# A selective-scan kernel: pair sums one step later, and loop rounds of four chunks in place of two

## What is computed

```python
def step(hst, inputs):
    ut, dt, bt, ct = inputs
    dA = jnp.exp(dt[..., None] * A)
    hst = hst * dA + (dt * ut)[..., None] * bt[:, :, None, :]
    y = jnp.einsum('bkdn,bkn->bkd', hst, ct)
    return (hst, y)
```

## Time and profile before

| | us |
|---|---|
| median of 3 runs | 35231.98 |
| their range | 35160.76 to 35288.79 |
| the profiled execution | 35258.12 |
| span of its trace | 35256.3 |
| the four scans in it, together | 21998 |

### The profile page before, as it was taken

One profiled execution on the slowest core, in us unless ns is written; L12 is line 12 of the kernel. 1 busy time (PEld: TensorE's weight loads), 2 busy tenths in 40 slices (PEclk: granted clock), 3 DMA queues, 4 the chain that ended last, 5 costly groups with the idle time before them and its releaser, 6 DMA issues. The chain is left out here.

```text
span 35256.3 us, 353348 instructions
## 1 busy us (share of the span) xinstructions
PE 26406.9 (75%) x100774; PEld 8372.0 (24%) x100774; DVE 24871.2 (71%) x15541; ACT 15127.5 (43%) x20404; POOL 21995.5 (62%) x9902
## 2 busy tenths in 40 slices
PE   7857888885547788888876668888873758888884
PEld 3422222221223322222223222222211322222221
DVE  1237999997322289999981269999983139999995
ACT  1044555553233345555511345555541245555551
POOL 0016999996000089999930149999980029999991
PEclk8857888887667778888867668888876768888887
DMA  1022122213212222221243221222124232122214
GB/s 67 10 116 77 40 48 47 48 42 102 80 67 96 97 52 48 48 47 40 47 151 122 105 87 43 44 47 45 42 61 159 94 110 44 43 47 48 47 42 147
DMA packets 928980, 2422.06 MB, mean 69 GB/s; under 512 B 113744, under 2 KB 331668, under 8 KB 919504
## 3 DMA queue, kind: packets, MB, share of 16 engines
q1 hardware_dynamic: 927000, 2398.76, 24.4%
HBM read 1375.34 MB, written 1023.05 MB: 68 GB/s over the span
## 5 line engine op out<-in xcount | busy, mean ns | idle before, releaser
L1086 POOL TENSOR_TENSOR scan_hc<-scan_bc,scan_h 128x1024 f32<-128x1024 f32 x6912 | 16089.6, 2352 | 716.1 <-DVE scan_h L1248 712.5
L1248 DVE TENSOR_TENSOR_SCAN scan_h<-scan_da,scan_state,scan_dbu 128x1024 f32<-128x1024 f32 x6912 | 15983.3, 2335 | 246.4 <-ACT scan_da L1138 237.8
L1169 PE MATMUL scan_da<-scan_dd,scan_ssel 32*128 32x512 f32 x27648 | 9456.1, 776 | 2807.7 <-DVE scan_h L1248 2610.9
L1138 ACT ACTIVATE scan_da<-scan_da,scan_a_cur 128x1024 f32<-128x1024 f32 x6912 | 7517.9, 1088 | 8291.5 <-PE scan_da L1169 8286.9
L1169 PE MATMUL scan_p_du<-scan_dd,scan_ssel 32*128 32x512 f32 x27648 | 9670.6, 781 | 657.9 <-DMA scan_bc<-bc_d 197.7
L1235 DVE TENSOR_TENSOR scan_dbu<-scan_p_du,scan_bc 128x1024 f32<-128x1024 f32 x4608 | 5553.9, 1205 | 1008.8 <-PE scan_p_du L1169 986.4
L1072 POOL TENSOR_TENSOR scan_dbu<-scan_bc,scan_dus 128x1024 f32<-128x1024 f32 x2304 | 5420.9, 2353 | 154.5 <-ACT scan_dus L1112 148.4
L1169 PEld LDWEIGHTS scan_da<-scan_dd,scan_ssel 32*128 32x128 f32 x27648 | 2562.4, 224 | 10345.9 <-DVE scan_h L1248 8310.3
L1186 PE MATMUL scan_p_y<-scan_hc,scan_rsel 128*32 128x512 f32 x27648 | 4930.3, 795 | 6.7 <-POOL scan_hc L1086 6.7
L1169 PEld LDWEIGHTS scan_p_du<-scan_dd,scan_ssel 32*128 32x128 f32 x27648 | 2491.8, 219 | 3817.4 <-DVE scan_dbu L1235 2937.0
L856 PE MATMUL prep_p_dt<-prep_dtv,prep_wdt 12*128 12x384 f32 x2304 | 1449.3, 789 | 1930.7 <-DVE prep_delta L914 1730.8
(11 more groups left out here) (202 smaller groups left out, 13865.8 us busy)
## 6 DMA issues: line engine op xcount, KB each, us to landing
scan_bc<-bc_d SPq DMA_DIRECT2D x576, 512.0 KB, 12.3
du_d<-prep_du SPq DMA_DIRECT2D x384, 576.0 KB, 2.8
delta_d<-prep_delta SPq DMA_DIRECT2D x384, 576.0 KB, 3.7
scan_dd<-delta_d SPq DMA_DIRECT2D x1152, 192.0 KB, 4.8
scan_dd<-du_d SPq DMA_DIRECT2D x1152, 192.0 KB, 6.6
y_d<-scan_y SPq DMA_DIRECT2D x576, 384.0 KB, 5.1
merge_y<-y_d SPq DMA_DIRECT2D x384, 576.0 KB, 3.8
xs_d<-proj_xs_o SPq DMA_DIRECT2D x96, 588.0 KB, 3.4
```

The source lines that it names most:

```text
L1086: nc.gpsimd.tensor_tensor(hc[:, u % HC_SLOTS, :], c, h[:, u % H_SLOTS, :], ALU.mult).then_inc(hc_ready, 1)
L1138: nc.scalar.activation(da[u % DELTA_BANKS][:], da[u % DELTA_BANKS][:], ACT.Exp, scale=a_cur[:, u // UNITS, u % UNITS:u % UNITS + 1]).then_ ...
L1169: return nc.tensor.matmul(dst[:, half * H:(half + 1) * H], ssel[rows, i, :], dd[rows, s, m, j, :], start=True, stop=True)
L1248: nc.vector.tensor_tensor_scan(h[:, v % H_SLOTS, :], da[v % DELTA_BANKS][:], dbu[:, v % DBU_SLOTS, :], state[:, v % UNITS:v % UNITS + 1], ...
```

## The change

The length of a round goes from two chunks to four, while the input slots stay two under a name of their own. `SUM_LAG` goes from 8 to 9, and PE sums pairs at odd steps: at step `u` the pair `u - 9, u - 8`. SP's loop still handles two chunks in a pass.

```diff
-UNROLL = 2
+UNROLL = 4
+CHUNK_SLOTS = 2
...
-SUM_LAG = 8
+SUM_LAG = 9
...
-        dd = ph.sb("dd", [P, UNROLL, TILES, BLOCKS, H])
-        bc = ph.sb("bc", [P, UNROLL, 2 * IMAGES, T])
+        dd = ph.sb("dd", [P, CHUNK_SLOTS, TILES, BLOCKS, H])
+        bc = ph.sb("bc", [P, CHUNK_SLOTS, 2 * IMAGES, T])
...
+        TURNS = UNROLL // CHUNK_SLOTS
         def slot(u):
-            return u // UNITS % UNROLL, u // ROUND
+            c = u // UNITS
+            return c % CHUNK_SLOTS, c // CHUNK_SLOTS + 1
...
-                with sp.Fori(0, ROUNDS - 1) as i:
-                    for s in range(UNROLL):
+                with sp.Fori(0, (ALL_CHUNKS - CHUNK_SLOTS) // CHUNK_SLOTS) as i:
+                    for s in range(CHUNK_SLOTS):
...
-                        if u % UNITS == UNITS - 1 and not (last and u > UNITS):
+                        if u % UNITS == UNITS - 1 and not (last and u == ROUND - 1):
                             s, n = slot(u + TRIO)
-                            t.wait_ge(loaded[s], r * LOADS + (n + 1) * LOADS + ONE)
+                            t.wait_ge(loaded[s], r * (TURNS * LOADS) + n * LOADS + ONE)
...
-                        if u % PAIR == 0 and (u >= SUM_LAG or not first):
+                        if u % PAIR == 1 and (u >= SUM_LAG or not first):
                             reduce(r, u - SUM_LAG)
...
-                for u in range(ROUND - SUM_LAG, ROUND, PAIR):
+                for u in range(ROUND - SUM_LAG + 1, ROUND, PAIR):
                     reduce(ROUNDS - 1, u)
```

More of the change, by code:

```diff
@@ L987, in scan @@
         carry = ph.sb("carry", [P, ALL_CHUNKS])
-        a_cur = ph.sb("a_cur", [P, UNROLL, UNITS + 1])
+        a_cur = ph.sb("a_cur", [P, CHUNK_SLOTS, UNITS + 1])
         ssel = ph.sb("ssel", [P, PER_QUAD, P])
         rsel = ph.sb("rsel", [P, PER_QUAD, QUAD])
-        dd = ph.sb("dd", [P, UNROLL, TILES, BLOCKS, H])
-        bc = ph.sb("bc", [P, UNROLL, 2 * IMAGES, T])
+        dd = ph.sb("dd", [P, CHUNK_SLOTS, TILES, BLOCKS, H])
+        bc = ph.sb("bc", [P, CHUNK_SLOTS, 2 * IMAGES, T])
         dus = ph.sb("dus", [P, DUS_SLOTS, T])
@@ L1004, in scan @@
         a_ready = ph.sem("a_ready")
-        loaded = [ph.sem(f"loaded{s}") for s in range(UNROLL)]
+        loaded = [ph.sem(f"loaded{s}") for s in range(CHUNK_SLOTS)]
         delta_spread = ph.sem("delta_spread")
@@ L1051, in store @@
                                          y[half * 64:(half + 1) * 64, b::2, :]).then_inc(y_stored, 16)
-                for s in range(UNROLL):
+                for s in range(CHUNK_SLOTS):
                     load(s * T, s)
-                with sp.Fori(0, ROUNDS - 1) as i:
[L1056 to L1061, removed]
+                with sp.Fori(0, (ALL_CHUNKS - CHUNK_SLOTS) // CHUNK_SLOTS) as i:
+                    for s in range(CHUNK_SLOTS):
+                        store(i * CHUNK_SLOTS + s, i * (CHUNK_SLOTS * T) + s * T)
+                        load(i * (CHUNK_SLOTS * T) + (s + CHUNK_SLOTS) * T, s)
+                for s in range(CHUNK_SLOTS):
+                    store(ALL_CHUNKS - CHUNK_SLOTS + s, (ALL_CHUNKS - CHUNK_SLOTS + s) * T)
                 sp.wait_ge(y_stored, STORES * ALL_CHUNKS + ONE)
@@ L1070, in share @@
                     g.sem_inc(passed, 1)
-                    s = u // UNITS % UNROLL
+                    s, _ = slot(u % ROUND)
                     nc.gpsimd.tensor_tensor(dbu[:, u % DBU_SLOTS, :], bc[:, s, image(u % UNITS), :],
@@ L1084, in rounds @@
                             g.wait_ge(reduced, nth(r * (ROUND // PAIR), (u - HC_SLOTS) // PAIR + 1) + ONE)
-                        c = bc[:, u // UNITS, IMAGES + image(u % UNITS), :]
+                        c = bc[:, slot(u)[0], IMAGES + image(u % UNITS), :]
                         nc.gpsimd.tensor_tensor(hc[:, u % HC_SLOTS, :], c, h[:, u % H_SLOTS, :],
@@ L1114, in keep @@
                 def keep(r, u):
-                    v, s = u % ROUND, u // UNITS % UNROLL
+                    v, s = u % ROUND, u // UNITS % CHUNK_SLOTS
                     a.wait_ge(scanned, r * ROUND + (u + 1) + ONE)
@@ L1138, in rounds @@
                         nc.scalar.activation(da[u % DELTA_BANKS][:], da[u % DELTA_BANKS][:], ACT.Exp,
-                                             scale=a_cur[:, u // UNITS, u % UNITS:u % UNITS + 1]).then_inc(da_ready, 1)
+                                             scale=a_cur[:, slot(u)[0], u % UNITS:u % UNITS + 1]).then_inc(da_ready, 1)
                         if u % EIGHT == 0 and (u >= 2 * EIGHT or not first):
                             evacuate(r, u // EIGHT - 2)
-                        if u % UNITS == UNITS // 2 and not (last and u > UNITS):
+                        if u % UNITS == UNITS // 2 and not (last and u > ROUND - UNITS):
                             chunk = r * UNROLL + (u // UNITS + 1)
-                            constants_of(chunk, (u // UNITS + 1) % UNROLL)
+                            constants_of(chunk, (u // UNITS + 1) % CHUNK_SLOTS)
                 a.wait_ge(consts, 64 + ONE)
@@ L1166, in spread @@
                 def spread(dst, n, u, half):
-                    s, (m, j, i) = u // UNITS % UNROLL, unit(u % UNITS)
+                    s, (m, j, i) = u // UNITS % CHUNK_SLOTS, unit(u % UNITS)
                     rows = slice((2 * n + half) * QUAD, (2 * n + half + 1) * QUAD)
@@ L1229, in times_b @@
                     if u % UNITS == 0:
-                        d.wait_ge(loaded[u // UNITS], r * LOADS + LOADS + ONE)
+                        s, n = slot(u)
+                        d.wait_ge(loaded[s], r * (TURNS * LOADS) + n * LOADS + ONE)
                     d.wait_ge(du_spread, r * (ROUND // TRIO * 2) + (u // TRIO * 2 + u % TRIO + 1) + ONE)
                     d.wait_ge(scanned, nth(r * ROUND, u - DBU_SLOTS + 1) + ONE)
-                    nc.vector.tensor_tensor(dbu[:, u % DBU_SLOTS, :], p_du[:], bc[:, u // UNITS, image(u % UNITS), :],
+                    nc.vector.tensor_tensor(dbu[:, u % DBU_SLOTS, :], p_du[:], bc[:, slot(u)[0], image(u % UNITS), :],
                                             ALU.mult).then_inc(dbu_ready, 1)
```

## The result

The changed kernel takes 34615.46 us (median of 4 runs, 34604.69 to 34624.19) against 35206.53 us: 591 us less, a ratio of 0.9829 with a 95% interval from 0.981 to 0.9849. I had forecast 35025 us, within 34800 to 35200.

The account below looks back on a forecast made before the run. POOL, at 9.22 us a trio in the scans with DVE close behind, was taken as the bound. From 35232 us, 207 for fewer jumps and 0 for the later sums gave 35025 us, range 34800 to 35200.

Parts of the forecast that it names:

- What bounds the kernel: Four scans: POOL at 9.22 us a trio, DVE at 9.05; 21243 us at POOL's pace against 21998 taken.
- The jumps, 207 us: PE's loop jumping back: 36 fewer jumps at 5.74 us each, 207 us saved, bounds 135 to 310 us.
- The count: PE's "issue" waits before its p_du matmuls: 6 a scan in place of 15, at the same 2.1 us each.
- My sign that a stretch with a jump should still cost 5 to 6 us more than one without: Scans: 48 steps holding a jump should still cost 5 to 6 us more than 48 without.
- DVE gathers lead where no jump eats it: Long rounds: DVE gains 0.17 us a trio on POOL, 11 us over 192 steps before something takes it.
- The sums, 0 us: PE's sums one step later: gain at most 346 us, loss at most 559 us, taken as 0.
- My "at most", 1.20 us at each of 288 places: Step 16 of every 24: DVE's two idle times bound the gain from moving the sum, 346 us in all.
- The sign that I had named for this case: If moving the sum frees step 16, stretches without a jump get shorter than 150.2 us.
- the whole pattern is moved by three steps: PE's order in the trio: sums at steps 1, 3, 5 repeat the old six-step pattern, alone worth 0.
- The hidden wait of POOL: POOL's wait for later-freed hc slots stays hidden, by 0.66 us at the tightest.
- PE's wait for products: PE's wait for hc gets a step of slack, worth nothing: only 6.7 us idle in the whole kernel.
- The freed place: Rival: step 16, at ACT's copy of p_y, is freed as well, 200 us more, 34825 us; chance 0.20.

Follow-up runs that it names:

- the second of the four kernels: The kernel before with the sums at odd steps, 9 late, and rounds still of two chunks: 34835.12 us (0.9891).

## Why the prediction was wrong, step by step

- **What bounds the kernel.** Right. POOL's pace of 9.22 us a trio is the wall, and the four scans now take 21355 us against the 21243 I worked out for it.
- **The jumps, 207 us.** Right within what can be told: long rounds alone brought 167 us, and the interval of the ratio is 116 to 264 us. With the sums already parted they brought some 220, from the second of the four kernels to the changed one, which ran on different chips. The count came as forecast, 6 for 15; the gap is 2.62 us in place of 2.35, so it grew by 11% where the body doubled. My sign that a stretch with a jump should still cost 5 to 6 us more than one without holds where only the rounds are longer (5.5), and not in the changed kernel (2.96). That DVE gathers lead where no jump eats it fits, but shows only once the spells were gone.
- **The sums, 0 us.** This is the step that failed. Alone they brought 367 us. I had the place, the two idle times and their causes in the earlier trace rows, and set against the delay that goes the same delay that comes. That takes the delays as what they cost, and they are not: in the earlier trace rows 0.83 us at DVE is followed by 5.9 us at POOL. My "at most", 1.20 us at each of 288 places, ended at the second idle time, and the spell lies behind it. That its 346 us come near the measured 367 is luck: it is 87 places at 4.1 us and not 288 at 1.20. The steps of the earlier trace rows that I worked through are the start of a spell, as two good trios stand ahead of them and four slow ones behind; I stopped at step 19, before the first late product of POOL, at 4606.43. The sign that I had named for this case did come: stretches without a jump got shorter than 150.2 us.
- **That the whole pattern is moved by three steps and therefore worth 0, except against the period of eight.** Right as far as the runs can tell, and the exception was the whole of it: with the sums left where they were, moving the copy brought as much (384 us beside 367).
- **The hidden wait of POOL, and PE's wait for products.** Right: the seven-late, eight-late and nine-late sums differ by nothing that can be told.
- **The rivals.** The freed place was the right one. I gave it 0.20 and 200 us, where it brought 367. The row that should have raised both was one that I used for it: some 770 us of DVE's idle time lay away from the jumps. The earlier trace rows should have, too: 150.24 us for 48 steps against POOL's 147.5. That gap of 2.7 us, 144 times in the kernel, is an estimate of 390 us that no jump explains, and I never asked what caused it.

## What to carry to other kernels

Where two engines run within 2% of each other, price what disturbs them by the equal work at which nothing happens, and account for the whole gap to the slower engine's pace before pricing any edit at zero. Write out all periods of a software pipeline (here 2, 3 and 8 steps): what coincides every 24 steps on the tightest chain can cost more than the instruction that coincides. Here moving the sum by one step either way removed it, and so did moving the copy to the next step. Count a delay by how long the engines take to recover, not by the first wait that it causes.

## What the runs showed of the hardware

At the place shown, a pause of PE of 0.64 us in place of 0.19, with a sum at the lower clock ahead of both, went with a granted clock of 0.68 over the next 43 us and four slow trios; the good trios after them had 0.85. In the kernel before, all 76 such places had a pause of at least 0.63 us and a spell behind it, 41 of all 87 spells at this place were four trios long, and the shortest were one. It looks like an amplifier, in which the higher clock keeps PE ahead and a PE that is ahead keeps the higher clock. That the clock is the cause and not the companion was not tried, as nothing in the kernel sets it.

The gap at a jump back is 2.35 us of PE's time on average where the body holds 96 steps (60 gaps), and 2.62 us where it holds 192 (24 gaps).
